# A third block in HBM for the rows of slots 16 to 19, with the other rows loaded and added during the last slots

## The chip, the cores and the metric

The program runs on one core of one Trainium2 chip. The metric is the time on the device in microseconds (us); lower is better. The core has five engines with a program each: TensorE (PE) for matmuls, VectorE (DVE), ScalarE (ACT), GpSimd (POOL) and SyncE (SP), which here only issues DMAs. They wait for one another through semaphores. Transfers between HBM and the core's memory are carried by 16 DMA engines, whoever issues them.

## The reference

One block of a network: attention of 1024 query rows (32 sequences of 32) over a context, a second attention whose weights come from mean activations, and a mixture of experts. The change touches only the last part, which is, cut to what matters:

```python
def _L0_ffn_ref(x, gate_w, w1, w2, w3):
    scores = softmax(xf @ gate_w)                      # T = 1024 rows, E = 8 experts
    top_scores, top_idx = top_k(scores, 2)             # each row has a first and a second choice
    scale = zeros((T, E)).at[arange(T)[:, None], top_idx].set(top_scores)
    xs = scale.T[:, :, None] * xf[None, :, :]
    h = silu(einsum('etd,edh->eth', xs, w1)) * einsum('etd,edh->eth', xs, w3)
    return einsum('eth,ehd->etd', h, w2).sum(axis=0)
x = x + _L0_ffn_ref(_layernorm(x), ...)
```

Rows have 512 numbers in float32, so a tile of 128 rows is 256 KB and there are eight tiles (`TILES = 8`).

## The kernel before

The expert part works in 23 **slots** (`NS`) of 128 rows. All rows of one slot belong to one expert; `idx` holds the row of the HBM tensor `total` to which each result goes, and `idx_x` the token that it comes from. For each slot j, POOL gathers the 128 input rows (`gather(j)`, L610, from `x_rows` into `xg`, two buffers), PE turns them (L1851), multiplies them by w1 and w3 of the expert (12 matmuls into `pK`), turns the hidden rows (L1874) and multiplies them by w2 (6 matmuls into `pV` or `pP` by turns). ACT copies the 128x512 result into `y_sb` (L966, two buffers), and POOL scatters it into `total` with an add in the DMA (`scatter(j)`, L616). PE runs a slot's steps in a fixed order, written by hand: turn of slot i+1, hidden of i, hidden turn of i-1, output of i-2. In its loop POOL issues, for each i, `gather(i + 3)` and then `scatter(i - 2)`.

`total` has blocks of T = 1024 rows. Rows of a slot that stand for no token go to blocks 0 to 2. The second choices go to block 3 (`other_t`). The first choices go to block 4 (`total_t`), in which ACT has stored the residual stream x before. Blocks 0 to 3 (`blank`) are filled with zeros by SP during the first attention, 32 transfers of 256 KB (L396, L405), one beside each context load. One scatter never names a row twice, and first and second choices of a token lie in different blocks. Scatters of several slots can therefore be in flight at the same time, and they are: nothing makes one wait for another, but for `y_sb`, whose two buffers ACT reuses after the scatter before last has landed (`added`).

The last three slots (`LAST = 3`, slots 20 to 22) are not scattered. ACT and DVE keep their results as two parts in `y_p`, and PE adds them to the right rows by multiplying with a 0/1 matrix `tok_hot` that DVE makes (`last_rows`, L1889 and L1890), into eight PSUM tiles `p_fin`.

The end of the program: SP waits until scatters 0 to 19 have all landed (L466). It then issues eight loads of 512 KB, two for each pair of tiles: first choices with x (L468) and second choices (L469) into `fin`. POOL adds the two (L633, eight instructions), DVE adds the PSUM tile of the last slots (L1489, eight), SP stores the even tiles and ACT the odd ones.

## Time and profile before

| | us |
|---|---|
| median of 3 runs | 750.65 (749.28 to 753.72) |
| the profiled execution, its own time | 752.54 |
| its span, from the first to the last instruction | 750.8 |
| PE busy | 710.5 (95% of the span) |
| DVE busy | 491.3 (65%) |
| ACT busy | 442.1 (59%) |
| POOL busy | 240.8 (32%) |

The mean granted clock of TensorE in the profiled execution was 0.982 of full speed. DMA moved 75.21 MB, 100 GB/s over the span. Times in the views are counted from the start of the span. A busy share is an average over stages: what the last 30 us cost is to be read from the views of that stretch.

### The profile page before, as it was taken

The page shows a single profiled execution, that of the slowest core. Times are in us where ns is not written, and L with a number is a line of the kernel's source. Part 1 is how long each engine was busy: PE and PEld are TensorE (multiplying, and loading weights), DVE is VectorE, ACT ScalarE, POOL GpSimd, SP SyncE. Part 2 cuts the span into 40 slices and gives each one's busy share as a digit, 9 for nine tenths or more (in the row PEclk, how much of TensorE's full clock was granted, in tenths as well). Part 3 has the DMA queues.
Part 4 walks back from the last instruction along what each step waited for, and adds up shares of the span by engine and source line. Part 5 has one row for each costly group of instructions (what it writes and reads, how often), then busy time and mean ns, then how long its engine had stood idle before and what let it go on. Part 6 is the DMA issues. An engine that isn't in the chain of part 4 may idle for free.

```text
span 750.8 us, 14081 instructions
## 1 busy us (share of the span) xinstructions
PE 710.5 (95%) x4873; PEld 590.5 (79%) x4873; DVE 491.3 (65%) x902; ACT 442.1 (59%) x958; POOL 240.8 (32%) x209
## 2 busy tenths in 40 slices
PE   4899999999999999999999989999999939999996
PEld 3677888888888888888888877888778827887874
DVE  6766766675757667757576566967467765655573
ACT  4655675675656656856666666564554435555550
POOL 1462212121212122212121125744920023555535
PEclk9999999999999999999999999999999959999999
DMA  9941121212121212121212306540124546665558
GB/s 305 98 127 42 43 86 43 85 50 75 46 79 42 84 42 84 43 83 42 84 42 85 100 1 183 180 148 10 57 85 168 171 145 217 104 107 104 109 82 326
DMA packets 59672, 75.21 MB, mean 100 GB/s; under 512 B 8784, under 2 KB 33360, under 8 KB 59632
## 3 DMA queue, kind: packets, MB, share of 16 engines
q1 hardware_dynamic: 52032, 58.16, 25.9%
q0 software_dynamic: 4720, 11.27, 8.2%
q10 hardware_dynamic: 2880, 5.24, 1.9%
q8 instruction: 24, 0.39, 0.2%
q14 instruction: 16, 0.13, 0.1%
HBM read 54.75 MB, written 19.92 MB: 99 GB/s over the span
## 4 chain that ended last, share of the span: by engine, by line
PE 84%; DVE 6%; DMA 4%; ACT 3%; issue 2%; POOL 1%; SPq 0%; POOLq 0%; ACTq 0%; DVEq 0%
PE pK L32 41%; PE pV L32 11%; PE pP L32 9%; PE pV L1625 5%; PE pT L1526 4%; PE pT L1714 4%; PE pS L1669 2%; PE pP L1696 2%; PE pT L1851 1%; DMA big<-x_rows,idx_x 1%; DMA fin<-total 1%; PE pT L1506 1%; PE pS L1791 1%; DVE bst L995 1%; PE pS L1874 1%
## 5 line engine op out<-in xcount | busy, mean ns | idle before, releaser
L32 PE MATMUL pK<-parts 128*128 128x512 f32 x840 | 211.3, 399 | 1.5 <-POOL parts L576 1.5
L535 POOL TENSOR_TENSOR parts<-big,parts 128x1024 fp32r<-128x1024 f32 x32 | 77.7, 2429 | 311.4 <-ACT parts L762 311.4
L32 PEld LDWEIGHTS pK<-parts 128*128 128x128 f32 x840 | 152.0, 188 | 32.3 <-POOL parts L576 2.0
L1037 DVE TENSOR_TENSOR kn<-pK,head_rs 128x512 f32<-128x512 f32 x62 | 42.9, 692 | 58.3 <-ACT head_rs L676 58.3
L32 PE MATMUL pK<-w,lhs 128*128 x276 | 70.8, 406 | 0.9 <-issue 0.6
L32 PEld LDWEIGHTS pK<-w,lhs 128*128 128x128 f32 x276 | 51.4, 192 | 12.9 <-issue 2.8
L32 PE MATMUL pP<-pT,parts 128*128 128x256 f32 x384 | 52.0, 284 | 0.0
L1452 DVE TENSOR_TENSOR w_p<-big,w_p 128x1024 fp32r<-128x1024 f32 x22 | 27.0, 1225 | 37.7 <-ACT w_p L952 37.7
L610 POOL DMA_INDIRECT big<-x_rows,idx_x x23 | 26.8, 1166 | 76.8 <-DVE idx_x L1408 60.8
L1031 DVE TENSOR_REDUCE head_ss<-sq 128x8 f32<-128x512 f32 x62 | 42.5, 685 | 13.1 <-ACT sq L670 13.1
L670 ACT ACTIVATE sq<-pK 128x512 f32<-128x512 f32 x62 | 36.9, 595 | 23.1 <-PE pK L32 23.0
L32 PE MATMUL pV<-pT,parts 128*128 128x256 f32 x384 | 49.5, 278 | 0.0
L32 PEld LDWEIGHTS pP<-pT,parts 128*128 128x128 f32 x384 | 46.6, 188 | 3.5 <-issue 0.9
L788 ACT ACTIVATE pT<-pP 128x512 fp32r<-128x512 f32 x32 | 19.2, 599 | 50.4 <-PE pP L1696 50.3
L32 PEld LDWEIGHTS pV<-pT,parts 128*128 128x128 f32 x384 | 46.6, 188 | 0.0
L32 PE MATMUL pK<-w_a,xT 128*128 128x512 f32 x192 | 46.0, 393 | 0.0
L616 POOL DMA_INDIRECT total<-big,idx x20 | 31.7, 1587 | 41.8 <-ACT big L966 41.8
L1174 DVE TENSOR_TENSOR pT<-pP,pT 128x512 fp32r<-128x512 f32 x32 | 22.1, 692 | 31.3 <-ACT pT L788 31.3
L32 PEld LDWEIGHTS pK<-w_a,xT 128*128 128x128 f32 x192 | 35.8, 188 | 7.8 <-issue 0.2
L1026 DVE TENSOR_TENSOR parts<-pT,parts 128x512 fp32r<-128x512 f32 x62 | 39.7, 682 | 2.5 <-ACT parts L662 2.5
L762 ACT ACTIVATE parts<-big 128x1024 fp32r<-128x1024 f32 x31 | 32.7, 1055 | 8.0 <-PE pV L32 8.0
L1526 PEld LDWEIGHTS pT<-ident,big 128*128 128x128 f32 x248 | 26.6, 141 | 12.4 <-issue 12.4
(320 smaller groups left out, 1454.3 us busy)
## 6 DMA issues: line engine op xcount, KB each, us to landing
big<-in_ctx_dram SPq DMA_DIRECT2D x32, 512.0 KB, 3.8
total<-zero SPq DMA_DIRECT2D x32, 256.0 KB, 4.0
w_raw<-in_L_ffn_w_dram SPq DMA_DIRECT2D x16, 512.0 KB, 5.9
big<-in_L_ffn_w_dram SPq DMA_DIRECT2D x8, 512.0 KB, 4.7
fin<-total SPq DMA_DIRECT2D x8, 512.0 KB, 7.6
x_rows<-big ACTq DMA_DIRECT2D x8, 256.0 KB, 2.2
total<-big ACTq DMA_DIRECT2D x8, 256.0 KB, 2.4
big<-in_x_dram SPq DMA_DIRECT2D x1, 1536.0 KB, 9.8
```

The lines of the kernel that those rows point to most:

```text
L32: last = pe.matmul(out, lhs(a, c), rhs(b, c), start=start and c == first and n == 0, stop=stop and c == chunks - 1 and n == 2)
L535: nc.gpsimd.tensor_tensor(ctxN[:, u, LO], ctx_raw[:, u], ctxN[:, u, HI].bitcast(F32), ALU.subtract).then_inc(cn_lo, 1)
L616: nc.gpsimd.indirect_dma_start(total[:, :], bass.IndirectOffsetOnAxis(idx[:, j:j + 1], 0), y_sb[:, j % 2, :], None, bounds_check=5 * T - 1 ...
L670: act.activation(sq[:, t], pKV[t][:, :], ACT.Square).then_inc(k_sq, 1)
L762: act.activation(ctxN[:, u, HI], ctx_raw[:, u], ACT.Copy).then_inc(cn_hi, 1)
L1026: tt(ctxT[:, u, LO, :, t * P:(t + 1) * P], pTT[t][:, :, :], ctxT[:, u, HI, :, t * P:(t + 1) * P].bitcast(F32), ALU.subtract).then_inc(ctx_ ...
L1031: nc.vector.tensor_reduce(head_ss[:, t], heads(sq[:, t]), AX.X, ALU.add).then_inc(k_ss, 1)
L1037: tt(heads(kn[:, t]), heads(pKV[t][:, :]), per_head(head_rs[:, t]), ALU.mult).then_inc(k_n, 1)
L1452: tt(w2_buf(j)[:, LO], w2_all[:, bass.ds(e, 1)].rearrange("p e c n -> p (e c) n"), w2_buf(j)[:, HI].bitcast(F32), ALU.subtract).then_inc(w ...
L1526: last = pe.transpose(pTT[t][:, c, :], ctx_raw[:, u, t, c * P:(c + 1) * P], ident[:, :])
L1625: last = pe.matmul(o, weights, rows[:, e * C + c].rearrange("p b q -> p (b q)"), start=k == 0, stop=k == C, tile_position=(0, e * HD))
L1714: last = pe.transpose(pTT[t][:, c, :], kn[:, t, c * P:(c + 1) * P], ident[:, :])
```

## The change

- `total` gets a sixth block. Blocks 0 to 3 stay, the new block 4 (`late_t`) is zeroed too, and the first choices with x move to block 5. The 32 zero transfers are of 320 KB in place of 256 KB.
- DVE rewrites `idx` of slots 16 to 19 (`CUT = 16`) during slot 8 with two small instructions, so that all their rows that stand for a token, first and second choices alike, go to block 4.
- Since two of these slots can hold the two choices of one token, `scatter(j)` for j = 17, 18, 19 waits until scatter j-1 has landed.
- SP issues the eight loads of `total_t` and `other_t` earlier, a pair of them each time one of the scatters 15, 16, 17 and 18 has landed. POOL adds the first to the second choices between its last scatters: tiles 0 and 1 behind scatter 17, 2 and 3 behind scatter 18, 4 to 7 behind scatter 19.
- When scatters 18 and 19 have landed, SP issues four loads of 512 KB from block 4 into `fin_late` in the order tiles 0-1, 4-5, 2-3, 6-7. POOL adds `fin_late` for tiles 0 to 3, DVE for tiles 4 to 7, and DVE then adds the PSUM tiles as before.

```diff
...
     LAST = 3
+    CUT = 16
...
         tok_f = sb("tok_f", [P, LAST])
+        late_at = sb("late_at", [P, NS - LAST - CUT])
         tok_t = sb("tok_t", [P, LAST, TILES])
...
         fin = at("fin", [P, TOP_K, TILES, D], 0)
+        fin_late = at("fin_late", [P, TILES, D], 64 * KB)
         tok_hot = at("tok_hot", [P, LAST, TILES, P], 32 * KB, F32R)
...
         x_rows = nc.dram_tensor("x_rows", (T, D), F32, kind="Internal").ap()
-        total = nc.dram_tensor("total", (5 * T, D), F32, kind="Internal").ap()
+
+        total = nc.dram_tensor("total", (6 * T, D), F32, kind="Internal").ap()
         other_t = total[3 * T:4 * T, :].rearrange("(t p) d -> p t d", p=P)
-        blank = total[0:4 * T, :].rearrange("(t p) d -> p t d", p=P)
+        late_t = total[4 * T:5 * T, :].rearrange("(t p) d -> p t d", p=P)
+        blank = total[0:5 * T, :].rearrange("r d -> (r d)").rearrange("(n p c) -> p n c", n=B, p=P)
         x_rows_t = x_rows[0:T, :].rearrange("(t p) d -> p t d", p=P)
-        total_t = total[4 * T:5 * T, :].rearrange("(t p) d -> p t d", p=P)
+        total_t = total[5 * T:6 * T, :].rearrange("(t p) d -> p t d", p=P)
...
-            zeros_of_row = zero[:, :].unsqueeze(1).broadcast_to([P, C, P])
+            zeros_of_row = zero[:, :].unsqueeze(1).broadcast_to([P, 5, P])
             early = 2
...
             for t in range(2):
-                sp.dma_start(blank[:, t, :].rearrange("p (n c) -> p n c", n=C), zeros_of_row).then_inc(zeroed, 16)
+                sp.dma_start(blank[:, t, :].rearrange("p (n c) -> p n c", n=5), zeros_of_row).then_inc(zeroed, 16)
...
                     sp.dma_start(ctx_raw[:, u], src).then_inc(ctx_in[u], 16)
-                    sp.dma_start(blank[:, bass.ds(k * 2 + u + 2, 1), :].rearrange("p t (n c) -> p (t n) c", n=C),
+                    sp.dma_start(blank[:, bass.ds(k * 2 + u + 2, 1), :].rearrange("p t (n c) -> p (t n) c", n=5),
                                  zeros_of_row).then_inc(zeroed, 16)
...
+            sp.wait_ge(u_mm, CUT + 1)
+            sp.wait_ge(added[CUT % 2], 16 * (CUT // 2))
+            for t in range(0, TILES, 2):
+                j = CUT + t // 2 - 1
+                sp.wait_ge(added[j % 2], 16 * (j // 2 + 1))
+                sp.dma_start(fin[:, 0, t:t + 2, :], total_t[:, t:t + 2, :]).then_inc(fin_in[t // 2], 16)
+                sp.dma_start(fin[:, 1, t:t + 2, :], other_t[:, t:t + 2, :]).then_inc(fin_in[t // 2], 16)
+            sp.wait_ge(u_mm, NS - LAST)
             for u in range(2):
                 sp.wait_ge(added[u], 16 * ((NS - LAST + 1 - u) // 2))
-            for t in range(0, TILES, 2):
-                sp.dma_start(fin[:, 0, t:t + 2, :], total_t[:, t:t + 2, :]).then_inc(fin_in[t // 2], 16)
-                sp.dma_start(fin[:, 1, t:t + 2, :], other_t[:, t:t + 2, :]).then_inc(fin_in[t // 2], 16)
+            for t in (0, C, 2, C + 2):
+                sp.wait_ge(fin_in[t // 2], 64 + 32)
+                sp.dma_start(fin_late[:, t:t + 2, :], late_t[:, t:t + 2, :]).then_inc(fin_in[t // 2], 16)
             for t in range(0, TILES, 2):
...
             nc.gpsimd.iota(slot_at[:, :], [[P, NJ]], base=0, channel_multiplier=0, allow_small_or_imprecise_dtypes=True)
-            nc.gpsimd.iota(block_of[:, :, :], [[-T, TOP_K], [P, TILES]], base=4 * T, channel_multiplier=0, allow_small_or_imprecise_dtypes=True)
+            nc.gpsimd.iota(block_of[:, :, :], [[-2 * T, TOP_K], [P, TILES]], base=5 * T, channel_multiplier=0, allow_small_or_imprecise_dtypes=True)
             nc.gpsimd.iota(row_no[:, :], [[1, 1]], base=0, channel_multiplier=1, allow_small_or_imprecise_dtypes=True)
...
                 pool.wait_ge(y_set, j + 1)
+                if j == CUT:
+                    pool.wait_ge(tok_set, 2)
+                if j > CUT:
+                    pool.wait_ge(added[(j - 1) % 2], 16 * ((j - 1) // 2 + 1))
                 nc.gpsimd.indirect_dma_start(total[:, :], bass.IndirectOffsetOnAxis(idx[:, j:j + 1], 0),
-                                             y_sb[:, j % 2, :], None, bounds_check=5 * T - 1,
+                                             y_sb[:, j % 2, :], None, bounds_check=6 * T - 1,
                                              compute_op=ALU.add).then_inc(added[j % 2], 16)
...
                     scatter(i - 2)
-            for t in range(TILES):
-                pool.wait_ge(fin_in[t // 2], 64 + 32)
-                nc.gpsimd.tensor_tensor(fin[:, 0, t], fin[:, 0, t], fin[:, 1, t], ALU.add).then_inc(fin_sum, 1)
+                for t in range(TILES):
+                    if i - 2 == CUT + 1 + min(t // 2, NS - LAST - CUT - 2):
+                        pool.wait_ge(fin_in[t // 2], 64 + 32)
+                        nc.gpsimd.tensor_tensor(fin[:, 0, t], fin[:, 0, t], fin[:, 1, t], ALU.add).then_inc(fin_sum, 1)
+            for t in range(C):
+                pool.wait_ge(fin_in[t // 2], 64 + 48)
+                pool.wait_ge(fin_sum, TILES)
+                nc.gpsimd.tensor_tensor(fin[:, 0, t], fin[:, 0, t], fin_late[:, t], ALU.add).then_inc(fin_sum, 1)
...
                 if i == E:
+                    slots_late = slice(CUT, NS - LAST)
+                    ts(late_at[:, :], idx[:, slots_late], 3 * T, 4 * T, ALU.is_ge, ALU.mult).then_inc(tok_set, 1)
+                    dve.wait_ge(tok_set, 1)
+                    tt(idx[:, slots_late], late_at[:, :], idx_x[:, slots_late], ALU.add).then_inc(tok_set, 1)
                     ts(tok_f[:, :], idx_x[:, NS - LAST:NS], 1.0, None, ALU.mult).then_inc(tok_set, 1)
-                    dve.wait_ge(tok_set, 1)
+                    dve.wait_ge(tok_set, 3)
                     tt(tok_t[:, :, :], tok_f[:, :].unsqueeze(2).broadcast_to([P, LAST, TILES]),
...
                     n = i - (NS - 5)
-                    dve.wait_ge(tok_set, 2 + n)
+                    dve.wait_ge(tok_set, 4 + n)
                     tt(tok_hot[:, n], col[:, :].unsqueeze(1).broadcast_to([P, TILES, P]),
...
                 tt(y_p[:, n, LO], pY[(NS - LAST + n) % 2], y_p[:, n, HI].bitcast(F32), ALU.subtract).then_inc(y_lo, 1)
+            for t in range(C, TILES):
+                dve.wait_ge(fin_in[t // 2], 64 + 48)
+                dve.wait_ge(fin_sum, t + 1)
+                tt(fin[:, 0, t], fin[:, 0, t], fin_late[:, t], ALU.add).then_inc(tok_set, 1)
             for t in range(TILES):
-                dve.wait_ge(fin_sum, t + 1)
+                if t < C:
+                    dve.wait_ge(fin_sum, TILES + t + 1)
+                else:
+                    dve.wait_ge(tok_set, 4 + LAST + t - C + 1)
                 dve.wait_ge(fin_mm, t + 1)
...
                     pe.wait_ge(x_lo, NS)
-                    pe.wait_ge(tok_set, 2 + LAST)
+                    pe.wait_ge(tok_set, 4 + LAST)
                     for t in range(C):
```

How the instructions stand on three engines. `added0` and `added1` count landed scatters of even and odd slots, `w13_in0` to `w13_in3` are the semaphores called `fin_in` in the code, `y_set` counts ACT's copies of results.

POOL before, from gather 22 (`big<-x_rows`) to the end of its program; the three scatters in the second row are 17, 18 and 19:

```order
L610 DMA big<-x_rows,idx_x 128x512 [waits xg_t]
L616 DMA total<-big,idx 5120x512 [waits y_set] x3
L633 TENSOR_TENSOR fin<-fin 128x512 [waits w13_in0] x2
L633 TENSOR_TENSOR fin<-fin 128x512 [waits w13_in1] x2
L633 TENSOR_TENSOR fin<-fin 128x512 [waits w13_in2] x2
L633 TENSOR_TENSOR fin<-fin 128x512 [waits w13_in3] x2
```

POOL after, the same place:

```order
L624 DMA big<-x_rows,idx_x 128x512 [waits xg_t]
L634 DMA total<-big,idx 6144x512 [waits added0,y_set]
L652 TENSOR_TENSOR fin<-fin 128x512 [waits w13_in0] x2
L634 DMA total<-big,idx 6144x512 [waits added1,y_set]
L652 TENSOR_TENSOR fin<-fin 128x512 [waits w13_in1] x2
L634 DMA total<-big,idx 6144x512 [waits added0,y_set]
L652 TENSOR_TENSOR fin<-fin 128x512 [waits w13_in2] x2
L652 TENSOR_TENSOR fin<-fin 128x512 [waits w13_in3] x2
L656 TENSOR_TENSOR fin<-fin,fin_late 128x512 [waits fin_sum,w13_in0] x2
```

The four pairs of adds L633 stood behind the last scatter; they now stand between the scatters (L652), each scatter from 17 on waits for the one before it, and four adds of `fin_late` (L656) are new.

SP before, from the last weight loads to the first store:

```order
L451 DMA big<-in_L_ffn_w_dram 128x2x512 x3
L468 DMA fin<-total 128x2x512 [waits added1,added0]
L469 DMA fin<-total 128x2x512
L468 DMA fin<-total 128x2x512
L469 DMA fin<-total 128x2x512
L468 DMA fin<-total 128x2x512
L469 DMA fin<-total 128x2x512
L468 DMA fin<-total 128x2x512
L469 DMA fin<-total 128x2x512
L472 DMA out_dram<-fin 128x512 [waits fin_add] x4
```

SP after, the eight loads of `fin` and the four new ones:

```order
L476 DMA fin<-total 128x2x512 [waits added1,added0,u_mm]
L477 DMA fin<-total 128x2x512
L476 DMA fin<-total 128x2x512 [waits added0]
L477 DMA fin<-total 128x2x512
L476 DMA fin<-total 128x2x512 [waits added1]
L477 DMA fin<-total 128x2x512
L476 DMA fin<-total 128x2x512 [waits added0]
L477 DMA fin<-total 128x2x512
L483 DMA fin_late<-total 128x2x512 [waits added1,w13_in0,added0,u_mm]
L483 DMA fin_late<-total 128x2x512 [waits w13_in2]
L483 DMA fin_late<-total 128x2x512 [waits w13_in1]
L483 DMA fin_late<-total 128x2x512 [waits w13_in3]
```

One wait for all scatters stood ahead of eight loads. Now each pair of loads has its own wait for one scatter, and the wait for the last scatters stands ahead of four loads.

DVE before, after the last part of `y_p`:

```order
L1485 TENSOR_TENSOR y_p<-pV,y_p 128x512 [waits y_set]
L1489 TENSOR_TENSOR fin<-fin,pT 128x512 [waits fin_mm,fin_sum] x2
L1489 TENSOR_TENSOR fin<-fin,pK 128x512 [waits fin_mm,fin_sum] x2
L1489 TENSOR_TENSOR fin<-fin,pP 128x512 [waits fin_mm,fin_sum]
L1489 TENSOR_TENSOR fin<-fin,pS 128x512 [waits fin_mm,fin_sum] x2
L1489 TENSOR_TENSOR fin<-fin,pV 128x512 [waits fin_mm,fin_sum]
```

DVE after, the same place:

```order
L1512 TENSOR_TENSOR y_p<-pV,y_p 128x512 [waits y_set]
L1516 TENSOR_TENSOR fin<-fin,fin_late 128x512 [waits fin_sum,w13_in2] x2
L1516 TENSOR_TENSOR fin<-fin,fin_late 128x512 [waits fin_sum,w13_in3] x2
L1523 TENSOR_TENSOR fin<-fin,pT 128x512 [waits fin_mm,fin_sum] x2
L1523 TENSOR_TENSOR fin<-fin,pK 128x512 [waits fin_mm,fin_sum] x2
L1523 TENSOR_TENSOR fin<-fin,pP 128x512 [waits fin_mm,tok_set]
L1523 TENSOR_TENSOR fin<-fin,pS 128x512 [waits fin_mm,tok_set] x2
L1523 TENSOR_TENSOR fin<-fin,pV 128x512 [waits fin_mm,tok_set]
```

Four adds of `fin_late` (L1516) now stand ahead of the eight last adds.

## Rows read from the trace of the kernel before

**Rows 1.** The page, shares of the chain that ended last, by engine.

```profile
PE 84%; DVE 6%; DMA 4%; ACT 3%; issue 2%; POOL 1%; SPq 0%; POOLq 0%; ACTq 0%; DVEq 0%
```

**Rows 2.** The chain of waits at the end: start us, us, what.

```profile
724.10 0.61 ACT big L966
...
724.76 0.72 issue
725.48 4.52 DMA total<-big,idx
...
730.07 0.37 SPq L468
...
732.53 9.24 DMA fin<-total
...
741.84 2.53 POOL fin L633 x2
...
746.99 0.69 DVE fin L1489
```

**Rows 3.** Timeline of POOL: start us, us, instruction, [idle before]; scatters 15 to 18, gather 22.

```profile
706.33 1.59 POOL L616 DMA_INDIRECT total<-big,idx  x1 [2.29 <-ACT big L966]
...
711.12 1.59 POOL L616 DMA_INDIRECT total<-big,idx  x1 [1.83 <-ACT big L966]
713.01 1.82 POOL L610 DMA_INDIRECT big<-x_rows,idx_x  x1 [0.31 <-issue]
715.91 1.59 POOL L616 DMA_INDIRECT total<-big,idx  x1 [1.08 <-ACT big L966]
...
720.73 1.57 POOL L616 DMA_INDIRECT total<-big,idx  x1 [3.23 <-ACT big L966]
```

**Rows 4.** All scatters: us from issue to landing (min/median/max of 20).

```profile
DMA to landing us min/median/max: 4.5/4.8/5.0
```

**Rows 5.** First and second load of `fin`, issued 730.07 and 730.48: issue to landing.

```profile
DMA to landing us min/median/max: 3.8/4.2/4.6
```

**Rows 6.** Third and fourth load of `fin`, issued 730.99 and 731.50: issue to landing.

```profile
DMA to landing us min/median/max: 5.9/6.5/7.2
```

**Rows 7.** All gathers: us from issue to landing (min/median/max of 23).

```profile
DMA to landing us min/median/max: 3.6/4.3/6.6
```

**Rows 8.** The gather issued at 616.34: its issue and landing.

```profile
L610 POOL DMA_INDIRECT big<-x_rows,idx_x x1: 1013/1013/1013, 616.3 to 616.3; - x1
...
DMA to landing us min/median/max: 5.9/5.9/5.9
```

**Rows 9.** The two w2 loads (512 KB each) issued beside that gather.

```profile
L451 SPq DMA_DIRECT2D big<-in_L_ffn_w_dram x2: 368/419/470, 616.4 to 616.8; - x2
```

**Rows 10.** Windows: us, busy by engine, PEclk, DMA share, GB/s; a scatter alone, then loads.

```profile
722.50:725.00 2.50, 2.31 (x11) 1.64 (x10) 2.34 (x4) 1.60 (x4) 0.00 (x0) 1.00 0.80 104
...
732.00:744.00 12.00, 11.65 (x51) 9.20 (x49) 3.96 (x7) 0.60 (x1) 7.26 (x6) 1.00 1.02 378
```

**Rows 11.** DMA queues from 600 us on: packets, MB, share; q0 is POOL's, q1 SP's.

```profile
q0 software_dynamic: 4720, 11.27, 40.6%
q1 hardware_dynamic: 4928, 9.44, 17.3%
```

**Rows 12.** Timeline of PE: turn of slot 22, and the last matmul.

```profile
719.10 0.60 PE L1851 MATMUL pT<-ident,big 128*128 128x128 f32 x4
...
743.26 0.39 PE L1890 MATMUL pV<-y_p,tok_hot 128*128 128x512 f32 x1
```

**Rows 13.** Timeline of DVE: small instructions of slot 8, and the first of the last adds.

```profile
663.17 0.16 DVE L1473 TENSOR_SCALAR tok_f<-idx_x 128x3 f32<-128x3 uint32 x1
...
740.56 1.28 DVE L1489 TENSOR_TENSOR fin<-fin,pT 128x512 f32<-128x512 f32 x2 [4.71 <-PE pT L1890]
```

**Rows 14.** SP's longest waits: us in total, times, longest.

```profile
SPq L402 <- POOL parts L535: 324.1, 30, 18.0
```

**Rows 15.** The stores of the output: us from issue to landing (min/median/max of 8).

```profile
DMA to landing us min/median/max: 2.0/2.9/3.1
```

## Prediction

> **What bounds the kernel now.** I read the page's chain first: PE holds 84% of the chain that ended last [rows 1]. But this chain changes hands near the end, and the change sits there, so the chain in order of time is the view that decides. In it PE's work ends with the output of slot 19; then nothing of PE stands in it [rows 2]. ACT copies that result from 724.10 to 724.71, POOL needs 0.72 us from there until its scatter starts at 725.48, and the scatter lands 4.52 us later, at 730.00. SP issues the first load of `fin` at 730.07, the sixth load lands at 741.77 (732.53 + 9.24), POOL adds, DVE adds last from 746.99 to 747.68, and the span ends at 750.8, 3.1 us behind it, which is a store's landing [rows 2, 15]. PE's last matmul ends at 743.65 [rows 12]. So the last 25 us are scatter 19, 4 MB of loads behind it, adds, and a store. The change takes half of those loads from behind the scatter. What it can win is bounded by that stretch; what it can lose is a later landing of scatter 19, since everything behind that moves one for one.
>
> **The end behind the last scatter.** Let X be the issue of the first load that waits for scatter 19: 730.07 now. After the change four loads of 512 KB stand there, as large as the first four now, and they land as those did, at X+3.8, X+5.0 (0.41 + 4.6), X+6.8 (0.92 + 5.9) and X+8.7 (1.43 + 7.2) [rows 5, 6]. The last is tiles 6 and 7, which DVE adds itself. Two DVE adds are 1.28 us [rows 13] and with the wake-up 1.35: X+10.05. Then come the eight last adds; two start-to-start are 1.2, so eight are 4.9: X+14.95. POOL's four `fin_late` adds are 1.27 each (2.53 for two [rows 2]); tiles 0 and 1 are free from X+3.8 and done at X+6.35, tiles 2 and 3 land at X+6.8 and are done at X+9.4. They bind nothing. With the 3.1 us of a store the span ends at X+18.1. [...] With X as now, DVE's last adds could not start before PE's first finished tile (740.56 now [rows 13], against X+10.05 = 740.12), which costs 0.4: the end would be 748.6, a gain of 2.2 us. That is the most the change can win.
>
> **The new wait between the scatters.** Scatters start at 706.33, 711.12, 715.91, 720.73 and 725.48 [rows 3, 2], 4.8 us apart, the pace of PE. A scatter lands 4.8 us after its start, between 4.5 and 5.0 [rows 4]. One lands, then, as the next starts. Scatter 16, started at 711.12, lands at 715.92 if nothing else changes, and 17 may start only behind that. The start does not follow at once: between ACT's end and the scatter's start lie 0.72 us of issue, 0.75 with POOL's move [rows 2], and this stands behind the last wait, so it now follows the landing. The spacing grows from 4.8 to 4.8 + 0.75. In numbers: 17 starts 716.67 and lands 721.47, 18 starts 722.22 and lands 727.02, 19 starts 727.77 and, at 4.5 as now, lands 732.27. X is 2.3 later by serial order alone. Queued behind POOL's wait are only its own adds and the next scatter; ACT needs landing 16 before its copy of result 18 (about 719.3) and landing 17 before the copy of 19 (724.10), so it waits only if these slip by over 2.6 us.
>
> **The loads beside the scatters.** This is the term with the widest bounds. Alone, a scatter keeps the DMA engines busy for 0.80 of 2.5 us, 2.0 us of all sixteen, though it moves only 104 GB/s [rows 10]. A pair of loads is 1.05 MB, 2.8 us of all sixteen at 378 GB/s [rows 10]. The first pair is issued when scatter 15 lands (711.13), the same moment in which scatter 16 starts; the other three are issued when 16, 17 and 18 land, 0.75 us ahead of scatters 17, 18 and 19. No row shows a scatter beside a load. The lower bound for what a scatter loses is nothing: it leaves bandwidth unused. The nearest row is a gather, also indirect and also 256 KB, at 616.34, with two 512 KB loads issued at 616.4 and 616.8: it landed after 5.9 us [rows 8, 9], while the median gather takes 4.3 [rows 7]. That is +1.6. The slowest gather took 6.6, +2.3 [rows 7], the upper bound for each. I take +1.6 for scatter 16, which starts with its loads as that gather did, and +1.2 for 17, 18 and 19, whose loads have a lead of 0.75 us. Sum: 1.6 + 3.6 = 5.2, with 0 and 9.2 as ends.
>
> In the Trainium skill, "DMA: Bandwidth & Descriptors", section "Issuing engines are not separate DMA queues" speaks against this change: transfers started by different engines run on the same 16 DMA engines and interleave. The gather's row agrees with it, and by it the loads are moved under other transfers, not into free time.
>
> **The rest.** Gather 22 (starts 713.01, usual landing 717.3) stands beside the first pair; with +1.6 it lands at 718.9, ahead of PE's turn at 719.10 [rows 3, 7, 12], and with +2.3 PE would wait 0.5 us, which costs nothing, as the tail then waits for scatter 19. The early POOL adds, 2.55 us for a pair, fit between scatters that are 5.55 us or more apart, of which 1.6 are the scatter's own. The zero transfers grow by a quarter; SP waits 324 us in 30 times for POOL there [rows 14], over 10 us each time, and that wait covers it. If it did not, 64 KB at 100 GB/s would be 0.65 us each. The two small DVE instructions are like L1473, 0.16 us [rows 13], during slot 8, where DVE has idle time. Both count as nothing.
>
> **The sum.** Landing of scatter 19: 732.27 + 5.2 = 737.5; X = 737.55; the end at X + 18.1 = 755.6, against 750.8: +4.8 us. In short, the difference is the sum of what the four scatters lose, less 0.4. The profiled execution took 752.54, 1.9 over the median; I put the difference on the median: 750.65 + 4.8 = **755.5 us**.
>
> **The rivals.**
> *(a) The transfers share by turns.* POOL's queue has 4720 packets for 43 transfers, 110 each or 7 per DMA engine; SP's has 4928 for 20, 1.9 KB each, so a pair of loads is some 34 per engine in about 3.1 us, 0.09 each [rows 11, 5, 6]. If the two queues take turns, a scatter waits for 7 load packets: 0.65 us. Four times that is 2.6, less 0.4: +2.2, 752.9 us. For it speaks that a scatter leaves two thirds of the bandwidth; against it that the gather, with as many packets, lost 1.6 and not 0.65. The page of the Trainium skill named above says, in "Queues, rings and completion order", that each DMA engine goes round the queues one packet at a time; by that rule this rival would be right, and the gather's row doesn't bear it out.
> *(b) Serial order alone.* The loads disturb nothing: -0.4, 750.3 us.
> *(c) The other side, faster.* A scatter that starts on an idle queue lands sooner than one that is issued while the last one drains: the spacing stays at 4.8, because landings fall from 4.8 to 4.05, and X stays at 730.07. The gain is the 2.2 of above: 748.5 us. It decides at a delay of X of 2.6 us: below that the change wins. For it: the last scatter took 4.5. Against it: all 20 lie between 4.5 and 5.0 [rows 4], and 2.3 of the 2.6 are spent by serial order.
> *(d) The change does not do what it says,* and the early loads wait for something late: then they stand in front of the four late ones, and the end is that of now plus the two megabytes more, 5.6 us: about 756 us. SP's order of waits speaks against it.
>
> **How the numbers follow.** A measurement of this kernel tells 0.5%, 3.75 us, from no change (746.9 to 754.4). The forecast, with a total loss over 4.15 us at the four scatters, has 0.47; (a), with a loss between 1 and 4.15, 0.33; (b) 0.08; (c) 0.05; (d) 0.02; something that no row shows, as a shift of a stage by the larger zero transfers, 0.05, taken as faster by over 0.5%, since every other case of gain stays within it. So slower 0.49, same 0.46, faster 0.05. The range reaches down past (b), to 750.0, and up to 759.0, near the upper bound of the loads' term (750.65 + 8.8 = 759.5).
>
> **What would show it.** In the profile after: scatters 17, 18 and 19 start later than 715.9, 720.7 and 725.5 and further apart than 5.5 us, each 0.75 us behind a landing; the landings from issue are 6.0 to 6.4 for 16 to 19 (5.5 by rival (a), 4.8 by (b), about 4.0 by (c)); scatter 19 lands near 737.5 and the first `fin_late` load is issued there; from it to the end are 18.1 us; PE ends as now. The forecast is wrong if the landings beside loads stay under 5.8, if POOL's 0.75 us are hidden behind the wait, or if the four late loads take under 8 us.

## The result, and the profile after

The changed kernel is slower by 1.0%: 758.22 us (median of 4 runs, 757.05 to 759.45) against 749.96 before (median of 4, 749.25 to 753.72); the ratio is 1.0101, with a 95% interval of 1.0080 to 1.0122. The prediction was 755.5, range 750.0 to 759.0, slower by over 0.5% with a chance of 0.49. Direction and the main mechanism were right, the size was short: +8.3 between the medians (+7.6 by the ratio) against +4.8.

The profiled execution took 757.05 us; the first line of its page:

```profile
span 754.9 us, 14109 instructions
```

The spans differ by 4.1 us, but scatter 15, from which the change acts, starts at 706.33 before [rows 3] and at 703.10 after: 3.2 us of difference lie ahead of the change, and runs of one kernel spread as much. So the ends are compared from the start of scatter 15: it was 44.5 us from there to the end (750.8 - 706.33), it is now 51.8 (754.9 - 703.10), **+7.3 us**.

The chain of waits after (start us, us, what), for [rows 2]:

```profile
707.89 7.15 DMA total<-big,idx
715.15 0.77 issue
715.92 5.87 DMA total<-big,idx
721.88 0.29 ACT big L989
...
724.74 3.08 issue
727.82 1.21 DVE w_last L1475
729.03 0.41 DVE sq L1465
...
744.35 0.36 issue
744.71 1.26 DVE fin L1516
```

Two things stand in it that were not there: scatters 16 and 17, which land after 7.15 and 5.87 us, and a stretch through DVE's part of w2 (`w_last`) back to PE. The second is not what the end waits for. The chain goes over from PE to an add of `fin_late` at 744.71, but that add waits for `fin_sum` and a load and for nothing of PE, so this link is not a wait. PE was done before DVE's first last add began at 746.98; its two waits for DVE and its last matmul:

```profile
723.04 3.00 PE L32 MATMUL pK<-w,lhs 128*128 x12 [1.80 <-DVE lhs L1459]
...
729.48 0.44 PE L1908 MATMUL pS<-ident,sq 128*128 128x128 f32 x2 [1.84 <-DVE sq L1465]
...
743.96 0.39 PE L1924 MATMUL pV<-y_p,tok_hot 128*128 128x512 f32 x1
```

What the end waits for is scatter 19 (729.32 + 5.8 = 735.1), the first late load at 735.27, the late loads and the adds.

POOL after, for [rows 3]; scatters 15 to 19, gather 22 and POOL's adds:

```profile
703.10 1.59 POOL L634 DMA_INDIRECT total<-big,idx  x1 [1.84 <-ACT big L989]
...
707.89 1.59 POOL L634 DMA_INDIRECT total<-big,idx  x1 [1.84 <-ACT big L989]
...
715.92 1.59 POOL L634 DMA_INDIRECT total<-big,idx  x1 [4.32 <-DMA total<-big,idx]
717.01 3.06 POOL L652 TENSOR_TENSOR fin<-fin 128x512 f32<-128x512 f32 x2
722.68 1.57 POOL L634 DMA_INDIRECT total<-big,idx  x1 [2.60 <-ACT big L989]
723.74 3.06 POOL L652 TENSOR_TENSOR fin<-fin 128x512 f32<-128x512 f32 x2
729.32 1.56 POOL L634 DMA_INDIRECT total<-big,idx  x1 [2.52 <-DMA total<-big,idx]
...
740.00 5.90 POOL L656 TENSOR_TENSOR fin<-fin,fin_late 128x512 f32<-128x512 f32 x4 [3.65 <-DMA fin_late<-total]
```

Scatters were 4.8 us apart. From 16 on they start at 707.89, 715.92, 722.68 and 729.32, that is 8.0, 6.8 and 6.6 apart. Scatter 18 is put down to ACT, not to the landing of 17: ACT's copy of result 19 waits for its buffer until scatter 17 has landed, and the two are released together. The landings of scatters 17 to 19 (us from issue, min/median/max; they were 4.5 to 5.0 [rows 4]):

```profile
DMA to landing us min/median/max: 5.8/5.8/5.9
```

DVE after, for [rows 13]; its instructions on w2 in the last slots and the adds of `fin_late`:

```profile
713.09 1.23 DVE L1475 TENSOR_TENSOR w_p<-big,w_p 128x1024 fp32r<-128x1024 f32 x1 [1.11 <-ACT w_p L975]
...
717.89 3.28 DVE L1475 TENSOR_TENSOR w_p<-big,w_p 128x1024 fp32r<-128x1024 f32 x1 [1.11 <-ACT w_p L975]
...
723.73 4.17 DVE L1475 TENSOR_TENSOR w_p<-big,w_p 128x1024 fp32r<-128x1024 f32 x1
...
741.29 5.76 DVE L1516 TENSOR_TENSOR fin<-fin,fin_late 128x512 f32<-128x512 f32 x4 [4.91 <-POOL fin L656]
746.98 1.27 DVE L1523 TENSOR_TENSOR fin<-fin,pT 128x512 f32<-128x512 f32 x2
```

This was not foreseen. The same instruction takes 1.23 us at 713.09, 3.28 at 717.89 and 4.17 at 723.73. The two slow ones stand beside POOL's adds, which run from 717.01 to 720.07 and from 723.74 to 726.80, and both end 1.1 us behind POOL: 721.17 and 727.90. DVE got nothing done while POOL added, and then did its own work. The four adds of `fin_late` on DVE take 1.44 us each on average beside POOL's four, which take 1.47; alone they are 0.65 and 1.27.

In the Trainium skill, "SBUF — State Buffer", section "Who interferes with whom", states that a DVE instruction with two SBUF inputs and a GpSimd instruction that reads SBUF exclude each other, and that the order of issue decides which of them waits. The rows above agree on the exclusion. On the order they say less: the two instructions at 723.73 and 723.74 began together, and in "no order, adds behind" below DVE began 0.57 us ahead of POOL's first add and waited all the same (spans on POOL are rough). The prediction did not use this, and the trace of before holds no POOL add beside such a DVE instruction in the slots.

### The profile page after: what moved, and what is told of

It is laid out like the page before. It is cut to its first block, busy times and chain, and to the rows that moved or that the text cites. A ratio compares the mean times of both kernels' runs of the same rounds, so it can differ in the third digit from the quotient of the medians.

```text
span 754.9 us, 14109 instructions
## 1 busy us (share of the span) xinstructions
PE 707.6 (94%) x4873; PEld 588.1 (78%) x4873; DVE 500.8 (66%) x908; ACT 441.9 (59%) x958; POOL 246.3 (33%) x213
## 3 DMA queue, kind: packets, MB, share of 16 engines
q1 hardware_dynamic: 57216, 62.36, 27.9%
## 4 chain that ended last, share of the span: by engine, by line
PE 84%; DVE 7%; ACT 3%; DMA 3%; issue 2%; POOL 0%; ACTq 0%; DVEq 0%; POOLq 0%
PE pK L32 41%; PE pV L32 11%; PE pP L32 8%; PE pV L1659 5%; PE pT L1560 4%; PE pT L1748 4%; PE pS L1703 2%; PE pP L1730 2%; DMA total<-big,idx 2%; PE pT L1885 1%; PE pT L1540 1%; PE pS L1825 1%; DVE bst L1018 1%; DVE fin L1523 1%; DVE head_mean L1038 1%
## 5 line engine op out<-in xcount | busy, mean ns | idle before, releaser
L1475 DVE TENSOR_TENSOR w_p<-big,w_p 128x1024 fp32r<-128x1024 f32 x22 | 32.0, 1453 | 36.6 <-ACT w_p L975 36.5
L811 ACT ACTIVATE pT<-pP 128x512 fp32r<-128x512 f32 x32 | 19.1, 598 | 50.5 <-PE pP L1730 50.4
L785 ACT ACTIVATE parts<-big 128x1024 fp32r<-128x1024 f32 x31 | 32.7, 1055 | 7.5 <-PE pV L32 7.5
L1560 PEld LDWEIGHTS pT<-ident,big 128*128 128x128 f32 x248 | 26.6, 141 | 12.4 <-issue 12.4
```

Source lines behind the costliest of these rows:

```text
L785: act.activation(ctxN[:, u, HI], ctx_raw[:, u], ACT.Copy).then_inc(cn_hi, 1)
L1475: tt(w2_buf(j)[:, LO], w2_all[:, bass.ds(e, 1)].rearrange("p e c n -> p (e c) n"), w2_buf(j)[:, HI].bitcast(F32), ALU.subtract).then_inc(w ...
L1560: last = pe.transpose(pTT[t][:, c, :], ctx_raw[:, u, t, c * P:(c + 1) * P], ident[:, :])
```

## The experiments

Three questions: what do the new waits cost without the loads, what do the loads cost without the waits, and does the exclusion of POOL and DVE matter for the end? "T" is the time from the start of scatter 15 in the profiled execution; X is the issue of the first load that waits for scatter 19.

| kernel | median us (before, same chip) | ratio, 95% interval | scatter 19 lands | X to end | end |
|---|---|---|---|---|---|
| before | - | - | T+23.7 | 20.7 | T+44.5 |
| changed | 758.22 (749.96) | 1.0101, 1.0080 to 1.0122 | T+32.0 | 19.6 | T+51.8 |
| order alone | 754.67 (751.14) | 1.0042, 1.0027 to 1.0058 | T+27.3 | 21.9 | T+49.3 |
| no order | 755.50 (751.14) | 1.0062, 1.0046 to 1.0079 | T+26.6 | 21.0 | T+47.8 |
| adds behind | 758.75 (751.14) | 1.0092, 1.0071 to 1.0113 | T+32.7 | 19.1 | T+51.9 |
| interleaved | 757.31 (751.14) | 1.0077, 1.0060 to 1.0094 | T+32.3 | 16.6 | T+49.1 |
| `fin_late` on DVE | 757.19 (751.34) | 1.0077, 1.0057 to 1.0097 | T+31.8 | 18.0 | T+50.0 |
| half loads | 752.87, one run (751.34) | - | T+27.9 | 19.0 | T+47.0 |
| behind and interleaved | 756.57 (751.34) | 1.0077, 1.0055 to 1.0098 | T+32.1 | 19.0 | T+51.2 |
| even and odd blocks | 750.43 (751.34) | 1.0004, 0.9988 to 1.0021 | T+27.3 | 16.2 | T+43.5 |
| no order, adds behind | 762.10 (750.99) | 1.0145, 1.0116 to 1.0174 | T+24.9 | 30.0 | T+54.9 |
| even and odd, two loads | 750.73 (750.99) | 0.9997, 0.9984 to 1.0010 | T+25.7 | 18.8 | T+44.6 |

**Order alone.** The kernel before, and only this:

```diff
             def scatter(j):
                 pool.wait_ge(y_set, j + 1)
+                if j > 16:
+                    pool.wait_ge(added[(j - 1) % 2], 16 * ((j - 1) // 2 + 1))
```

> The kernel before with one edit: scatters 17, 18 and 19 wait until the scatter before them has landed; no third block, no early loads. Theory (each wait costs the issue time behind it, 0.85 us, and the loads cost the rest): scatters start 5.6 to 5.7 us apart, land 4.8 after their start, from the start of scatter 15 to the landing of 19 it is 23.7 + 2.6 = 26.3 us, and the time is 2.6 us over before. Rival (a landing that is waited for costs more than the row says, and serial order is most of the loss): 5 us or more over before, with landings over 5 us.

Measured +0.42%, 3.2 us, between the two expectations and nearer the first. Scatter 19 lands 3.6 us later than before, not 2.6. (The profiled execution is the slowest of the seven, 758.95 us against a median of 754.67, so its end, T+49.3, overstates the loss: the last of the eight loads lands 15.6 us behind X there, against 14.3 before.) POOL shows two sizes that were off:

```profile
712.73 1.59 POOL L618 DMA_INDIRECT total<-big,idx  x1 [1.83 <-ACT big L968]
...
718.50 2.12 POOL L618 DMA_INDIRECT total<-big,idx  x1 [2.06 <-DMA total<-big,idx]
724.61 1.94 POOL L618 DMA_INDIRECT total<-big,idx  x1 [3.99 <-DMA total<-big,idx]
730.53 1.55 POOL L618 DMA_INDIRECT total<-big,idx  x1 [3.97 <-DMA total<-big,idx]
```

The starts are 5.8, 6.1 and 5.9 apart, and the issue on POOL took 2.12 and 1.94 us in place of 1.59, with landings of 5.2, 5.1 and 4.7. Both longer issues began while DVE ran instructions with two SBUF inputs; this row of DVE in the same kernel covers the first:

```profile
717.93 1.22 DVE L1454 TENSOR_TENSOR w_p<-big,w_p 128x1024 fp32r<-128x1024 f32 x1 [1.10 <-ACT w_p L954]
```

**No order.** The changed kernel without the waits; `idx` of slots 16 to 19 is set to rows of blocks 0 to 2 that nothing else uses.

```diff
-                if j > CUT:
-                    pool.wait_ge(added[(j - 1) % 2], 16 * ((j - 1) // 2 + 1))
...
-                    ts(late_at[:, :], idx[:, slots_late], 3 * T, 4 * T, ALU.is_ge, ALU.mult).then_inc(tok_set, 1)
+                    ts(late_at[:, :], slot_row[:, slots_late], 1.0, None, ALU.mult).then_inc(tok_set, 1)
                     dve.wait_ge(tok_set, 1)
-                    tt(idx[:, slots_late], late_at[:, :], idx_x[:, slots_late], ALU.add).then_inc(tok_set, 1)
+                    tt(idx[:, slots_late], late_at[:, :], slot_row[:, slots_late], ALU.max).then_inc(tok_set, 1)
```

> The changed kernel with one edit that lets the waits between scatters go: the rows of slots 16 to 19 are sent to rows of blocks 0 to 2 that no other slot uses, so no two scatters name the same row, and scatters 17 to 19 wait for nothing but their result. The contributions of these slots are left out of the output. Early loads and late loads are as in the changed kernel. Theory (loads and serial order both cost): landings of 16 to 19 stay at 5.8 to 7.2 us beside the loads, starts are 4.8 to 5.5 us apart, scatter 15's start to 19's landing is 25.5 to 27 us in place of 32.1, and the time is 0 to 2 us over before. Rival (all is DMA congestion): without the order the transfers pile up, landings grow to 8 us and more, and the time stays near that of the changed kernel, 7 us over before.

Scatter 19 lands at T+26.6, inside 25.5 to 27, and the transfers don't pile up: landings are 4.6 to 7.2. But the time is +0.62%, 4.7 us, more than either part of the expectation allows for, though less than the rival's 7. What holds up the end is no longer the scatter alone. In this kernel POOL's adds fell on the next DVE instruction on w2, and PE waited. The first last add then waits for PE, 13.1 us behind X:

```profile
725.28 3.96 DVE L1473 TENSOR_TENSOR w_last<-big,w_last 128x1024 fp32r<-128x1024 f32 x1
```

```profile
729.69 0.44 PE L1906 MATMUL pS<-ident,sq 128*128 128x128 f32 x2 [3.16 <-DVE sq L1463]
```

```profile
742.76 1.28 DVE L1521 TENSOR_TENSOR fin<-fin,pT 128x512 f32<-128x512 f32 x2 [0.43 <-PE pT L1922]
```

A second thing made PE late here, which the expectation did not have. Behind the wait of 3.16 us the granted clock of TensorE fell to 0.50, the lower of its two levels (1.2 GHz), while in the changed kernel, behind waits of 1.80 and 1.84 us, it stayed at 1.00. The window 732 to 734.5 us of this kernel, then 731 to 734 of the changed one (us, busy by engine, granted clock, DMA share, GB/s):

```profile
732.00:734.50 2.50, 2.50 (x7) 1.93 (x8) 0.69 (x1) 0.56 (x1) 2.26 (x2) 0.50 1.01 365
```

```profile
731.00:734.00 3.00, 2.93 (x14) 2.10 (x13) 1.08 (x2) 0.60 (x1) 2.62 (x3) 1.00 1.06 296
```

A step of `last_rows` took 0.43 us there in place of 0.23. At half speed 2.5 us of PE's work cost 1.25 us more, an estimate from these rows. "Interleaved", "`fin_late` on DVE" and "no order, adds behind" have such a stretch too.

The same kernel shows that DVE is not always shut out of a pair of POOL adds. This time it came in between them: it ended 1.1 us behind the first add, and the second add waited for it.

```profile
713.61 4.38 POOL L650 TENSOR_TENSOR fin<-fin 128x512 f32<-128x512 f32 x2
```

```profile
714.53 2.32 DVE L1505 TENSOR_TENSOR tok_hot<-col,tok_t 128x1024 fp32r<-128x1024 f32 x1
```

**Adds behind.** The changed kernel with POOL's eight adds behind its last scatter.

```diff
-                for t in range(TILES):
-                    if i - 2 == CUT + 1 + min(t // 2, NS - LAST - CUT - 2):
-                        pool.wait_ge(fin_in[t // 2], 64 + 32)
-                        nc.gpsimd.tensor_tensor(fin[:, 0, t], fin[:, 0, t], fin[:, 1, t], ALU.add).then_inc(fin_sum, 1)
+            for t in range(TILES):
+                pool.wait_ge(fin_in[t // 2], 64 + 32)
+                nc.gpsimd.tensor_tensor(fin[:, 0, t], fin[:, 0, t], fin[:, 1, t], ALU.add).then_inc(fin_sum, 1)
```

> The changed kernel with POOL's eight adds of first and second choices moved back behind scatter 19, as they stood before. Theory (POOL's adds block DVE's instructions with both inputs in SBUF): the DVE low parts of w2 in the last slots fall from 3.3 and 4.2 us to 1.23, PE's waits of 1.8 us in slots 21 and 22 go and PE ends 3 to 3.6 us sooner; since scatter 19's landing sets the end, the time changes by less than 1.5 us. Rival (PE's delay is what the tail waits for): 3 us faster than the changed kernel. Second rival (DVE was slowed by the DMA traffic): the DVE instructions stay at 3 to 4 us.

DVE in the slots is back to its old time, with the loads still beside it, which rules out the DMA traffic as the cause:

```profile
720.31 1.22 DVE L1474 TENSOR_TENSOR w_p<-big,w_p 128x1024 fp32r<-128x1024 f32 x1 [0.79 <-ACT w_p L974]
...
726.75 1.23 DVE L1474 TENSOR_TENSOR w_p<-big,w_p 128x1024 fp32r<-128x1024 f32 x1 [2.76 <-ACT w_p L974]
```

PE's last matmul ends 38.8 us behind the start of scatter 15 in place of 41.3, and the time did not move (1.0092 against 1.0101). That agrees with the reading above: in the changed kernel itself PE's delay was not what the end waited for. By itself this run would not show it, since the eight adds moved into the tail stand in the way of `fin_late` there, and scatter 17 landed 0.7 us later.

**Interleaved.** The changed kernel with another order on DVE, and stores in the order of the last adds.

```diff
...
+            late_add(4)
+            late_add(5)
+            for t in (0, 1, 4, 5):
+                last_add(t)
+            late_add(6)
+            late_add(7)
+            for t in (6, 7, 2, 3):
+                last_add(t)
```

> The changed kernel with the order of DVE's last instructions changed: fin_late of tiles 4 and 5, last adds of 0, 1, 4, 5, fin_late of 6 and 7, last adds of 6, 7, 2, 3, and the stores in that order. Theory (all eight last adds wait for the last late load): with only six adds behind that load the end comes 3 to 4 us sooner, some 754.5 us. Rival (the stores bind): under 1.5 us.

From X to the end it is 16.6 us, 3.0 less, as expected, and now PE is what DVE waits for: its last matmul starts at 749.23, 9.9 us behind X. A part of that is again the clock, 0.54 of full speed from 734 to 737 us. By the medians the gain is 0.9 us, by the ratios 0.24% with intervals that overlap. So the time missed the expected 3 to 4 us and is as small as the rival's, but for another reason than the stores.

**`fin_late` on DVE.** POOL's last loop goes, and DVE adds `fin_late` of all tiles in the order in which they land.

```diff
-            for t in range(C):
-                pool.wait_ge(fin_in[t // 2], 64 + 48)
-                pool.wait_ge(fin_sum, TILES)
-                nc.gpsimd.tensor_tensor(fin[:, 0, t], fin[:, 0, t], fin_late[:, t], ALU.add).then_inc(fin_sum, 1)
...
+            late_order = (0, 1, 4, 5, 2, 3, 6, 7)
+            for t in late_order:
...
```

> The changed kernel with the four fin_late adds of POOL given to DVE, so that POOL adds nothing while DVE adds fin_late. Theory (two adds with all inputs in SBUF block each other on DVE and POOL): the DVE adds of fin_late take 0.64 us each in place of 1.44, the last add starts some 10.1 us behind the issue of the first late load in place of 11.7, and the time is 1 to 1.6 us under the changed kernel's although DVE does four adds more. Rival (they were slowed by the loads that still arrive): the adds stay over 1 us each and the time is 2 us or more over the changed kernel's.

```profile
741.72 2.59 DVE L1513 TENSOR_TENSOR fin<-fin,fin_late 128x512 f32<-128x512 f32 x4 [1.66 <-DMA fin_late<-total]
745.18 2.57 DVE L1513 TENSOR_TENSOR fin<-fin,fin_late 128x512 f32<-128x512 f32 x4 [0.87 <-DMA fin_late<-total]
747.67 1.28 DVE L1517 TENSOR_TENSOR fin<-fin,pT 128x512 f32<-128x512 f32 x2
```

Eight adds at 0.65 on one engine are done sooner than four and four on two: the last adds start 10.1 us behind X (737.60), against 11.7 in the changed kernel. The rival falls: the adds are at their old time with the same loads beside them. The time is 1.0 us under the changed kernel's by the medians, the lower end of what was expected, with intervals that overlap.

**Half loads.** The early load of second choices is cut to 16 partitions, and POOL's adds read the first choices twice.

```diff
-                sp.dma_start(fin[:, 1, t:t + 2, :], other_t[:, t:t + 2, :]).then_inc(fin_in[t // 2], 16)
+                sp.dma_start(fin[0:16, 1, t:t + 2, :], other_t[0:16, t:t + 2, :]).then_inc(fin_in[t // 2], 16)
...
```

> The changed kernel with the early load of second choices cut from 128 partitions (512 KB) to 16 (64 KB), so that beside each of scatters 16 to 19 stand 576 KB in place of 1 MB. The second choices of slots 0 to 15 are left out of the output, POOL's adds read the first choices twice. Theory (a scatter waits for the load bytes that are queued with it): the losses shrink with the bytes that the load has left, scatter 16 to some 5.9 us from 7.2 and scatters 17 to 19 to 5.0 to 5.2 from 5.8. Rival (the queues take turns, so a scatter loses the same beside any load that is long enough): 16 stays over 6.5 and the others at 5.6 to 5.8.

The landings of scatters 16 to 19 (min/median/max), where 16 is the 5.6:

```profile
DMA to landing us min/median/max: 4.9/5.0/5.6
```

7.2 became 5.6, and 5.8 became 4.9 to 5.0. Against 4.8 (4.5 for the last) the losses are 0.7 us and 0.2 to 0.3 us. What a scatter loses goes with the bytes beside it: the first theory. This rests on four scatters of one execution.

**Behind and interleaved.** Both edits at once, with the last adds in the order 4, 5, 6, 7, 0, 1, 2, 3. Against "interleaved":

```diff
-                for t in range(TILES):
-                    if i - 2 == CUT + 1 + min(t // 2, NS - LAST - CUT - 2):
-                        pool.wait_ge(fin_in[t // 2], 64 + 32)
-                        nc.gpsimd.tensor_tensor(fin[:, 0, t], fin[:, 0, t], fin[:, 1, t], ALU.add).then_inc(fin_sum, 1)
+            for t in range(TILES):
+                pool.wait_ge(fin_in[t // 2], 64 + 32)
+                nc.gpsimd.tensor_tensor(fin[:, 0, t], fin[:, 0, t], fin[:, 1, t], ALU.add).then_inc(fin_sum, 1)
...
-            for t in (0, 1, 4, 5):
+            for t in (4, 5):
                 last_add(t)
             late_add(6)
             late_add(7)
-            for t in (6, 7, 2, 3):
+            for t in (6, 7, 0, 1, 2, 3):
                 last_add(t)
```

> The changed kernel with both edits: POOL's eight adds of first and second choices behind scatter 19, and DVE's order fin_late of 4 and 5, last adds of 4 and 5, fin_late of 6 and 7, last adds of 6, 7, 0, 1, 2, 3, with the stores in that order. Theory (the interleaved version was held up by PE, which DVE's blocked instructions had delayed): PE ends 6 us behind the first late load in place of 10, and the time is 3 us under the changed kernel's, 1 us under the interleaved one's; still 4 us over before, since the scatters' order and the loads beside them stay. Rival (POOL's adds, now all behind scatter 19, bind): no better than the interleaved version.

PE's last matmul does end 6.0 us behind X, as expected, with the clock at 1.00. But the rival was right on the time, 1.0077 as "interleaved". POOL's eight adds now reach far into the time of the late ones, and DVE's adds wait for them:

```profile
730.61 10.57 POOL L651 TENSOR_TENSOR fin<-fin 128x512 f32<-128x512 f32 x8
741.32 6.10 POOL L655 TENSOR_TENSOR fin<-fin,fin_late 128x512 f32<-128x512 f32 x4
```

```profile
744.62 3.34 DVE L1515 TENSOR_TENSOR fin<-fin,fin_late 128x512 f32<-128x512 f32 x2
```

**No order, adds behind.** The same edits together with those of "no order", which leave the contributions of slots 16 to 19 out of the output. Against "behind and interleaved":

```diff
-                if j > CUT:
-                    pool.wait_ge(added[(j - 1) % 2], 16 * ((j - 1) // 2 + 1))
...
-                    ts(late_at[:, :], idx[:, slots_late], 3 * T, 4 * T, ALU.is_ge, ALU.mult).then_inc(tok_set, 1)
+                    ts(late_at[:, :], slot_row[:, slots_late], 1.0, None, ALU.mult).then_inc(tok_set, 1)
                     dve.wait_ge(tok_set, 1)
-                    tt(idx[:, slots_late], late_at[:, :], idx_x[:, slots_late], ALU.add).then_inc(tok_set, 1)
+                    tt(idx[:, slots_late], late_at[:, :], slot_row[:, slots_late], ALU.max).then_inc(tok_set, 1)
```

> The version without order between the scatters (rows of slots 16 to 19 to unused rows, these contributions left out of the output) with POOL's eight adds behind scatter 19 and DVE's last adds interleaved. Theory (without order the end was held up by PE, which DVE's blocked instructions had delayed): DVE's parts of w2 are back at 1.23 us, scatter 19 lands some 25 to 26 us behind the start of scatter 15, the first late load is issued there, and the end follows 19 us later, 44 to 45 us behind the start of scatter 15: the time is within 1 us of before. So even without the order the change would win nothing, since what it saves behind the last scatter is paid beside the scatters. Rival (order was the only real cost): 2 us or more under before.

Scatter 19 landed at T+24.9, next to the 25 to 26 expected, and yet this is the slowest of all, +1.45%. Theory and rival both fall. Scatter 19 now starts early, so that POOL's row of adds begins while DVE still has two instructions on w2 to do:

```profile
724.76 1.55 POOL L632 DMA_INDIRECT total<-big,idx  x1 [3.62 <-ACT big L986]
725.79 7.92 POOL L649 TENSOR_TENSOR fin<-fin 128x512 f32<-128x512 f32 x6
```

```profile
725.22 9.58 DVE L1472 TENSOR_TENSOR w_p<-big,w_p 128x1024 fp32r<-128x1024 f32 x1 [1.53 <-ACT w_p L972]
```

```profile
736.39 0.69 PE L1915 MATMUL pS<-ident,sq 128*128 128x128 f32 x2 [8.64 <-DVE sq L1462]
```

An instruction of 1.23 us took 9.58: DVE did not get in between six adds of POOL that stood in a row, and PE waited 8.64 us. Behind that wait PE went on at a granted clock of 0.50 until about 740 us. So whether the changed tail without order would beat the kernel before stays open; this run does not answer it.

**Even and odd blocks.** The kernel before with another use of its two blocks, which needs neither a third block nor a new wait between scatters.

```diff
-            nc.gpsimd.iota(block_of[:, :, :], [[-T, TOP_K], [P, TILES]], base=4 * T, channel_multiplier=0, allow_small_or_imprecise_dtypes=True)
+            nc.gpsimd.iota(block_of[:, :, :], [[0, TOP_K], [P, TILES]], base=3 * T, channel_multiplier=0, allow_small_or_imprecise_dtypes=True)
...
+                if i == 0:
+                    even = idx[:, :].rearrange("p (n u) -> p n u", u=2)[:, :, 0]
+                    ts(even_at[:, :], even, 3 * T, T, ALU.is_ge, ALU.mult).then_inc(tok_set, 1)
+                    dve.wait_ge(tok_set, 1)
+                    tt(even, even, even_at[:, :], ALU.add).then_inc(tok_set, 1)
...
+            for u, block in enumerate((total_t, other_t)):
+                sp.wait_ge(added[u], 16 * ((NS - LAST + 1 - u) // 2))
+                for t in range(0, TILES, 2):
+                    sp.dma_start(fin[:, u, t:t + 2, :], block[:, t:t + 2, :]).then_inc(fin_in[t // 2], 16)
...
```

> A version of the kernel before without a third block and without new waits: rows of even slots, first and second choices alike, go to the block that holds x, rows of odd slots to the other one. Two scatters into one block are two slots apart, and the second starts only when ACT has refilled its buffer, which already waits for the first to land. The even block is complete when scatter 18 has landed, 4.8 us before 19, so its four loads are issued there, and only the four loads of the odd block stand behind scatter 19. POOL adds tiles 0, 1, 4 to 7, DVE 2 and 3. Theory: scatter 19 lands 1 to 2.4 us later beside the loads, the last load lands 3 to 4 us sooner than before, DVE's eight last adds behind PE's first tile bind, and the time is 1 to 2.2 us under before. Rival (the loss of scatter 19 beside 2 MB of loads is larger than the time won): within 0.5 us of before or slower.

Beside 2 MB of loads scatter 19 took:

```profile
DMA to landing us min/median/max: 8.1/8.1/8.1
```

That is +3.6, more than the 2.4 expected. The end in the profiled execution is 1.0 us nearer than before (T+43.5), but 12 runs show no difference: ratio 1.0004, 0.9988 to 1.0021. The rival was right: what scatter 19 loses eats up what the earlier loads win.

**Even and odd, two loads.** Two of the four early loads are moved behind scatter 19, and DVE adds tiles 6 and 7. Against "even and odd blocks":

```diff
-            for u, block in enumerate((total_t, other_t)):
+            for u, pairs in enumerate((((0, 0), (0, 2)), ((1, 0), (1, 2), (0, 4), (1, 4), (0, 6), (1, 6)))):
                 sp.wait_ge(added[u], 16 * ((NS - LAST + 1 - u) // 2))
-                for t in range(0, TILES, 2):
-                    sp.dma_start(fin[:, u, t:t + 2, :], block[:, t:t + 2, :]).then_inc(fin_in[t // 2], 16)
+                for v, t in pairs:
+                    sp.dma_start(fin[:, v, t:t + 2, :], (total_t, other_t)[v][:, t:t + 2, :]).then_inc(fin_in[t // 2], 16)
...
-            for t in (0, 1, 4, 5, 6, 7):
+            for t in range(6):
                 pool.wait_ge(fin_in[t // 2], 64 + 32)
...
```

> The version with blocks by even and odd slots, with two of its four early loads (1 MB in place of 2 MB) issued when scatter 18 has landed and the other two behind scatter 19, among those of the odd block; POOL adds tiles 0 to 5, DVE 6 and 7 after four last adds. Theory (a scatter's loss goes with the bytes queued beside it): scatter 19 lands in 5.8 us in place of 8.1, as beside 1 MB in the changed kernel. The end is 43 to 44 us behind the start of scatter 15, against 43.5 and 44.5 of before, and the time 0 to 1.5 us under before. Rival (a fixed cost of any load beside it): over 7 us.

```profile
DMA to landing us min/median/max: 6.5/6.5/6.5
```

Between theory and rival. Together with the changed kernel, its variants that keep the order, and the half loads, it gives one scatter's loss as 0.2 to 0.3 us beside 0.6 MB that have a lead and 0.7 beside 0.6 MB without one, 1.0 to 1.7 beside 1 MB with a lead (1.7 and 1.5 are scatter 17 in "adds behind" and "interleaved", which landed after 6.5 and 6.3 us), 2.0 to 2.4 beside 1 MB without one, and 3.6 beside 2 MB. The time is that of before, 0.9997 (0.9984 to 1.0010).

## Why the prediction was right, and where it was short

- **What bounds the end.** Right: the end moved with scatter 19, and PE's delay did not count, though "PE ends as now" was wrong: PE ends 41.3 us behind the start of scatter 15 in place of 37.3.
- **The new wait.** The mechanism was right, the size a little short. The gaps between a landing and the next start are 0.88, 0.89 and 0.84 us, not 0.75: between +0.3 and +0.4 in all. Order alone costs 3.2 us by the ratio (3.5 between the medians) where this term made 2.3, or 3.6 to the landing of scatter 19 in the profiled execution; some 0.9 of that are longer landings, their longer issues included, in the kernel without loads.
- **The loads beside the scatters.** Right, with the first scatter just over the upper bound of 2.3 taken for each. The sum taken was 5.2; measured are landings of 7.2, 5.9, 5.8 and 5.8, together 24.7 against 18.9, so 5.8. The first scatter lost 2.4 (I took 1.6), the others 1.1, 1.0 and 1.3 (I took 1.2 each). Rival (a), turns by packet at 0.65 each, fell; so did (b), with nothing lost, and (c). Rival (d) fell too: the early loads are issued at 708.18, 715.06, 721.81 and 728.50, each next to a landing. The half loads show the dependence on bytes that (a) would not have had for the first scatter; that the queues take turns in units of the 1.9 KB that (a) counts is shown by no run. There was some luck in the size: the +1.6 came from one gather beside two loads, while in the same trace a gather at 673.53 took 6.2 us with no load near it, so that row alone did not show what loads cost.
- **Gather 22.** Landing taken 5.9, measured 5.7 to 5.9 in the five kernels with the same loads whose traces have it (the changed kernel's own has none); PE did not wait for it.
- **The failed step: the end behind X.** The prediction made it 18.1 us, "X+10.05" for DVE's adds of `fin_late` and "They bind nothing" for POOL's. It is 19.6: the last late load lands 8.6 us behind X as expected (736.7 + 7.2 = 743.9), but DVE's four adds end at X+11.8, since they and POOL's block one another. With POOL out of the way all eight end at X+10.1 (`fin_late` on DVE). That is +1.7, and nearly all of it is left at the end: the eight last adds took 4.9 us and the store behind them 3.1, both as forecast.
- **"Small POOL adds fit between the scatters."** They fit on POOL, which is all that the prediction priced. They held up DVE by 2.0 and 2.9 us and PE by 1.8 twice. It was hidden only because the scatters were slower still; where they are not, PE sets the end ("no order", "no order, adds behind").
- **The sum.** By the traces: scatter 19 lands 8.4 us later (7.5 predicted), and X to the end is 1.1 shorter (2.6 predicted): 7.3 in place of 4.9, so the miss is 0.9 + 1.5. The medians differ by 8.3, inside the interval of the ratio (6.0 to 9.2 us). Some 0.3 us of the rest lie outside the span: time less span is 1.7 to 1.9 us in the runs of before and 2.1 to 2.2 in those of the changed kernel. What is left is spread that no trace here explains. The larger zero transfers show no cost, as taken: scatter 15 starts at 702.9 to 706.8 in the eight kernels that have them and at 704.4 to 707.9 in the four that do not.
- **The chances.** 0.46 on no change was too much. 0.33 of it stood on rival (a), which the one row on a gather beside loads spoke against, weak as that row was.

## What to carry to other kernels

Work moved beside a chain of latencies is paid on that chain: here 1 MB of loads beside each scatter cost 1.0 to 2.4 us each, together more than the 2 MB saved behind the last one. Before adding a wait between transfers, look for an order that exists already, as ACT's reuse of a buffer orders scatters two apart. An "idle" POOL is not free for elementwise work on SBUF: look at what DVE runs in that stretch, and keep long rows of POOL adds off any DVE instruction with two SBUF inputs that PE waits for; two engines adding by turns were slower than DVE alone.

## What the hardware showed that I had not expected

- POOL adds and DVE instructions with both inputs in SBUF did not overlap: 1.23 us became 3.28, 4.17 and, beside six POOL adds in a row, 9.58, each time ending 1.1 us behind the last of the adds. Once DVE came in between two adds (2.32 us, "no order"), and in the tail the two took turns; what decides this the runs do not show. DVE's last adds, with one input in PSUM, kept their 0.64 us.
- The issue of an indirect DMA on POOL grew too when it began beside such a DVE instruction: 2.12 and 1.94 us in "order alone", and 2.60 in "no order", in place of 1.59. Gather 22 shows it before too: it began beside a `tok_hot` of DVE and its issue took 1.82 us in place of 1.07 [rows 3].

```profile
718.15 2.60 POOL L632 DMA_INDIRECT total<-big,idx  x1 [0.17 <-issue]
```

- A scatter with add, which moves 104 GB/s alone [rows 10], was not carried beside loads for nothing: it lost 3.6 us beside 2 MB, which take 5.6 us at 378 GB/s.
- The granted clock of TensorE fell to 0.50 behind PE's waits of 3.16 us ("no order") and 8.64 ("no order, adds behind"). It also fell in "interleaved", with waits of 1.66 and 2.25, and in "`fin_late` on DVE", with 1.61 and 1.80, but not in the changed kernel, with 1.80 and 1.84. So a wait of PE near the end can cost more than its own length, and a comparison of two executions there needs the clock beside it.
